# Work moved ahead of its phase: cross-attention's weights and first context, soft MoE's first norms, and the shared expert's turned rows

## The reference, cut to what matters

```python
x = x + tanh(g_xattn[0]) * ssm_attention(ctx, ctx, layernorm(x))          # phase 1
# phase 2 and 3: eight routed experts (top 2) and one shared expert
xn = layernorm(x)
moe = sum over e of ce[e] * (silu(xn @ gate[e]) * (xn @ up[e])) @ down[e]
shared = silu(xn @ s_gate_w + b) * (xn @ s_up_w + b) @ s_down_w + s_down_b
x = x + tanh(g_ffn[0]) * (moe + shared)
# phase 4: linear cross-attention, 16 heads
q, k, v = f(xn @ Wq.T), f(ctx @ Wk.T), ctx @ Wv.T                          # f(x) = x + 1 if x > 0 else exp(x)
x = x + tanh(g_xattn[1]) * ((q @ (k.T @ v)) / (q . sum(k)) * sigmoid(xn @ Wg.T + bg)) @ Wo.T
# phase 5: soft MoE, 16 experts of 128 slots
x_ln = layernorm(layernorm(x)) * gamma + beta      # the outer norm is the layer's own
logits = (l2norm(x_ln) * scale) @ l2norm(mu);  dispatch, combine = softmax over tokens-slots
x = x + tanh(g_ffn[1]) * combine @ (gelu(dispatch.T @ x_ln @ W1 + b1) @ W2 + b2)
```

## Time and profile before

| what | us |
|---|---|
| median of three runs | 1786.04 (1781.75 to 1788.67) |
| the profiled execution | 1787.78 |
| its span | 1786.1 |
| shared expert, from the first to the last of its own matmuls | 252 to 479 |
| routed experts, PE | 493 to 731.5 |
| cross-attention, PE | 743.6 to 1091.5 |
| soft MoE, PE | 1110.5 to the end |
| PE busy over the span | 1571.0 |

### The profile page before, as it was taken

How to read it: one execution, slowest core, us unless ns; L and a number is a source line. 1 busy time by engine, 2 the same in 40 slices (tenths; PEclk the granted TensorE clock), 3 DMA queues, 4 the chain that set the end, 5 groups by cost and what they waited for, 6 DMA issues and landing times. The chain is left out here.

```text
span 1786.1 us, 27541 instructions
## 1 busy us (share of the span) xinstructions
PE 1571.0 (88%) x9532; PEld 915.7 (51%) x9532; DVE 1094.1 (61%) x2223; ACT 752.3 (42%) x1386; POOL 513.2 (29%) x426
## 2 busy tenths in 40 slices
PE   4989948999799999579888874969999999999997
PEld 3878833444356666335444441445555555555554
DVE  7998845345622322368685855665766767675663
ACT  5442214343213322244343431555575656565462
POOL 0658814322324433333443322101202020101101
PEclk8999979999899999789999996989999999999999
DMA  9544544333575765641524125542341505142341
GB/s 206 141 120 150 157 151 150 115 128 128 182 187 124 183 178 136 225 152 60 159 85 146 55 88 211 210 94 54 77 89 42 129 8 121 28 101 53 66 88 44
DMA packets 274043, 215.19 MB, mean 120 GB/s; under 512 B 184514, under 2 KB 222914, under 8 KB 272274
## 3 DMA queue, kind: packets, MB, share of 16 engines
q1 hardware_dynamic: 233696, 153.58, 32.7%
q10 hardware_dynamic: 30978, 30.06, 5.6%
q0 software_dynamic: 9264, 30.15, 5.5%
HBM read 120.33 MB, written 49.63 MB: 95 GB/s over the span
## 5 line engine op out<-in xcount | busy, mean ns | idle before, releaser
L2031 POOL TENSOR_TENSOR s_h_lo<-s_h,s_h_hi 128x512 f16<-128x512 f32 x32 | 36.9, 1154 | 550.3 <-DVE s_h_hi L2242 550.3
L1218 DVE TENSOR_TENSOR e_h<-e_up,e_silu 128x352 f32<-128x352 f32 x39 | 20.5, 525 | 151.4 <-ACT e_silu L1177 151.4
L2260 PE MATMUL s_ring<-w_mu,s_xt_hi 128*128 128x512 f16 x256 | 98.4, 384 | 3.4 <-DVE s_xt_lo L2163 3.0
L2168 DVE TENSOR_REDUCE s_top<-s_lg 128x1 f32<-128x512 f32 x64 | 43.9, 686 | 89.1 <-ACT s_lg L2074 88.9
L2261 PE MATMUL s_ring<-w_mu,s_xt_hi 128*128 128x512 f16 x256 | 98.3, 384 | 0.0
L2262 PE MATMUL s_ring<-w_mu,s_xt_lo 128*128 128x512 f16 x256 | 98.0, 383 | 0.0
L2260 PE MATMUL s_acc<-w_w,s_g_hi 128*128 128x512 f16 x256 | 97.2, 380 | 0.1
L2262 PE MATMUL s_ring<-w_w,s_xt_lo 128*128 128x512 f16 x256 | 97.2, 380 | 0.0
L2260 PE MATMUL s_ring<-w_w,s_xt_hi 128*128 128x512 f16 x256 | 97.2, 380 | 0.0
L2261 PE MATMUL s_ring<-w_w,s_xt_hi 128*128 128x512 f16 x256 | 97.2, 380 | 0.0
L2261 PE MATMUL s_acc<-w_w,s_g_hi 128*128 128x512 f16 x256 | 97.1, 379 | 0.0
(11 more groups left out here) (378 smaller groups left out, 4809.7 us busy)
## 6 DMA issues: line engine op xcount, KB each, us to landing
expert_rows<-e_y SPq DMA_DIRECT2D x39, 256.0 KB, 2.0
a_part_in<-in_L_ffn_W ACTq DMA_DIRECT2D x32, 256.0 KB, 3.2
w_split<-a_part_q ACTq DMA_DIRECT2D x32, 256.0 KB, 2.5
w_w<-w_split SPq DMA_DIRECT2D x8, 1024.0 KB, 16.1
toep<-ssm_split ACTq DMA_DIRECT2D x14, 512.0 KB, 5.4
stage<-in_L_ffn_gate_w SPq DMA_DIRECT2D x8, 704.0 KB, 4.5
stage<-in_L_ffn_up_w SPq DMA_DIRECT2D x8, 704.0 KB, 5.2
c_rows<-in_ctx SPq DMA_DIRECT2D x8, 512.0 KB, 11.4
```

What stands on the lines that cost most here:

```text
L2031: nc.gpsimd.tensor_tensor(hp[1][:, n % 2, :], h32[:, :], hp[0][:, n % 2, :], ALU.subtract).then_inc(S["h_lo"], 1)
L2168: V.tensor_reduce(top[:, t, j:j + 1], lg[:, t, j * D:(j + 1) * D], AX.X, ALU.max).then_inc(S["top_done"], 1)
L2260: mm(out_, a[0], b_[0], start=first, stop=False)
```

## The change

Five things.

1. Shared expert: chunk 0 is as before. For chunks 1 to 3 PE no longer turns the rows and ACT and DVE no longer split turned blocks. The rows are normed, split untransposed into `xq` right behind the norm, and SP turns both halves with four DMA transposes (`xq_turned`) into `xt` once the last gate/up of the chunk before is done (`gu_done`). The store of `xq` comes behind them. PE waits for `xq_turned` ahead of gate/up, and for `bias_added` where it writes `tr`.
2. Experts: wk, wv, wq, wg, wo are loaded, split and stored as float16 pairs (`xw_split`) in 20 parts, one on every odd tile: ACT issues its load, copies and stores it, DVE subtracts. At tile 19 SP loads the first context into a tile that outlives the phases (`k.ahead.home`). `PERIOD` is 7.
3. Cross-attention: no WS. SP loads the five split weights, 1 MB each, the second context between the third and the fourth. The gathers are first on POOL. PE follows `begin`, all other engines `beside`, up to the first Q.
4. Chunk 3's Q/G stage takes in the two norms of soft MoE's batch 0 (N1a to N3b; SP loads its rows, gamma, beta and scale once the last context is turned).
5. Soft MoE starts with X; the loads of rows, gamma, beta, scale and the operations of N2f are gone.

```diff
+            def store_xn(c):
+                sp.wait_ge(xq_lo_done, (c + 1) * 4)
+                sp.dma_start(xn_d[:, c * 4:c * 4 + 4, :], xq.rearrange("p t q d -> p t (q d)")).then_inc(xn_stored, 16)
...
+                    sp.wait_ge(gu_done, (c + 1) * SK)
+                    for t in range(4):
+                        sp.wait_ge(xq_lo_done, (c + 1) * 4 + t + 1)
+                        sp.dma_start_transpose(xt[:, :, t * P:(t + 1) * P], xq[:, t, :, :].rearrange("p q d -> p (q d)")).then_inc(xq_turned, 16)
+                    store_xn(c + 1)
...
+            def split_rows(c, t):
+                if not t and c:
+                    act.wait_ge(xn_stored, c * 16)
+                    act.wait_ge(xq_turned, (c - 1) * 4 * 16)
+                act.wait_ge(normed, c * 4 + t + 1)
+                nc.scalar.activation(xq[:, t, 0, :], xn[:, t, :], ACT.Copy).then_inc(xq_hi_done, 1)
...
+                            if m == 0 and o == 0 and c and b == 0:
+                                pe.wait_ge(xq_turned, c * 4 * 16)
...
-        PEEL, FIRST, PERIOD = 9, 4, 8
+        PEEL, FIRST, PERIOD = 9, 4, 7
...
+                i = part_at(n)
+                if i is not None:
+                    v = i % PART_BUFS
+                    act.wait_ge(part_loaded[v], (i // PART_BUFS + 1) * 16)
+                    if i >= PART_BUFS:
+                        act.wait_ge(part_stored[v], i // PART_BUFS * 16)
+                    nc.scalar.activation(part_q[:, v, 0, :], part_in[:, v, :], ACT.Copy).then_inc(part_hi, 1)
+                    if i >= 1:
+                        store_part(i - 1)
+                    if i >= 1 and i + 1 < PARTS:
+                        load_part(i + 1)
...
+                if n == TILES // 2:
+                    sp.wait_ge(w.x1s_stored, NCH * 16)
+                    sp.dma_start(k.ahead.home[:, :, :], ctx.rearrange("(c k p) d -> p (c k) d", p=P, k=4)[:, 0:4, :]).then_inc(k.ahead.ctx_loaded, 16)
...
+        begin = ops(0, "TC", 4) + key(0) + key(1) + key(2) + key(3) + ops(0, "TX", 4)
+        beside = (ops(0, "TC", 4) + mixed(ops(0, "CB", 4), key(0) + key(1)) + ops(0, "NA", 1) + ops(0, "NB", 1)
+                  + ops(0, "TX", 4) + key(2) + key(3))
+        first_norm = [(0, op, 0) for op in ("N1a", "N1b", "N2a", "N2b", "N3a", "N3b")]
...
-            sp.dma_start(ctx_in[:, :, :], ctx_d[:, 0:4, :]).then_inc(ctx_loaded, 16)
             sp.dma_start(bg[:, :], bg_cols).then_inc(small_loaded, 16)
+            for n in range(5):
+                if n == 1:
+                    load_rows(0)
+                if n == 3:
+                    load_next(0)
+                sp.dma_start(halves[n].rearrange("p q k d -> p (q k d)"), xw_split[n]).then_inc(w_loaded[n], 16)
...
+                if c == NCH - 2:
+                    sp.wait_ge(c_turned, NCH * 4)
+                    sp.wait_ge(stored, c * 4 * 16)
+                    sp.dma_start(ah.x_ln, x3_d[:, 0:2, :]).then_inc(AS["x_loaded"], 16)
+                    for dst, src in ((ah.gam, gamma), (ah.bet, beta), (ah.scl, scale)):
+                        sp.dma_start(dst[:, :], src.partition_broadcast(P)).then_inc(AS["small"], 16)
...
-        F1a, F1b, F2a, F2b, F3a, F3b = normalised(1)
-        before = (F1a + F1b + F2a + one("N2f", 0) + ops("X", 0, 2, 1) + F3a + F3b + ops("L", 0, 4, 1) + ...
+        before = (ops("X", 0, 2, 1) + ops("L", 0, 4, 1) + ...
```

More of the change, by code:

```diff
@@ L753, in _ @@
                         split_piece(c, m)
[L754 to L757, removed]
+                        if c == 0:
+                            split_rows(0, m)
                     act.wait_ge(h_done, n + 1)
@@ L1233, in background @@
             def background(n):
+                i = part_at(n)
+                if i is not None:
+                    v = i % PART_BUFS
+                    dve.wait_ge(part_hi, i + 1)
+                    nc.vector.tensor_tensor(part_q[:, v, 1, :], part_in[:, v, :], part_q[:, v, 0, :], ALU.subtract).then_inc(part_lo, 1)
                 j = quarter_at(n, 5)
@@ L1303, in xattn_phase @@
         ln = LayerNorm(sb, sem, "x2")
-        wq, wg, wkv, wo = (tuple(sb(f"{n}_{q}", [P, KD, m], F16) for q in ("hi", "lo"))
-                           for n, m in (("wq", D), ("wg", D), ("wkv", 2 * D), ("wo", D)))
-        stage = sb("a_stage", [P, 2, 2, 2 * D])
+        halves = [sb(f"a_{n}", [P, 2, KD, D], F16) for n in ("wk", "wv", "wq", "wg", "wo")]
+        wk, wv, wq, wg, wo = ((h[:, 0], h[:, 1]) for h in halves)
         bg = sb("a_bg", [P, KD])
         mask = sb("a_mask", [P, 2 * P])
-        ctx_in, x2 = sb("a_ctx", [P, 4, D]), sb("a_x2", [P, X_BUFS, 4, D])
+        ah, AS = k.ahead, k.ahead.S
+        ctx_in, x2 = ah.home, sb("a_x2", [P, X_BUFS, 4, D])
         y_in = sb("a_y", [P, 4, 2, D])
+        waste = y_in[:, 0, 0, :].bitcast(F16).rearrange("p (t d) -> p t d", t=2)
         xn = sb("a_xn", [P, 4, D])
@@ L1348, in xattn_phase @@
         x1s_d, x3_d, ctx_d = (a.rearrange("(c k p) d -> p (c k) d", p=P, k=4) for a in (x1s, x3, ctx))
-        pieces = [(m, dst, b) for m, dst in ((wkv_t, wkv), (wq_t, wq), (wg_t, wg), (wo_t, wo)) for b in (0, 2)]
-        NP = len(pieces)
-        def staged(n):
-            cols = pieces[n][1][0].shape[2]
-            return stage[:, n % 2, :, 0:cols]
         def ops(c, op, count):
@@ L1380, in xattn_phase @@
         parts = iter(range(PARTS))
-        schedule = [o for at in schedule for o in ([at, (0, "P", next(parts))] if at[1] == "QF" or at[1] == "AT" and at[2] % 2 else [at])]
+        steady = [o for at in schedule for o in ([at, (0, "P", next(parts))] if at[1] == "QF" or at[1] == "AT" and at[2] % 2 else [at])]
         assert next(parts, None) is None
+        schedule = begin + steady
         w1_d = w1.rearrange("(j e) (p k) h -> j k p e h", j=NJ, k=KD)
@@ L1400, in xattn_phase, with run @@
                 home[at] = home[at[0], SECOND[at[1]], at[2]]
-        def run(step):
-            for at in schedule:
+        def run(step, first=beside):
+            for at in first + steady:
                 step(*at, home.get(at))
@@ L1523, in step @@
                     A(xt[0][:, :, n * P:(n + 1) * P], ring[:, bank, :].rearrange("p (k i) -> p k i", i=P), ACT.Copy).then_inc(x_hi, 1)
-                if op == "WS":
-                    act.wait_ge(w_loaded[n % 2], (n // 2 + 1) * 16)
-                    _, dst, b = pieces[n]
-                    A(dst[0][:, b:b + 2, :], staged(n), ACT.Copy).then_inc(w_hi, 1)
                 if op == "NA":
                     ln.root(nc, act, c)
+                if op == "N1a":
+                    ah.ln1.root(nc, act, 0)
+                if op == "N2a":
+                    ah.ln2.root(nc, act, 0)
+                if op == "N3a":
+                    act.wait_ge(combined, NCH * 4)
+                    for t in range(2):
+                        act.wait_ge(AS["xln_done"], t + 1)
+                        A(waste[:, t, :], ah.x_ln[:, t, :], ACT.Square, accum_out=ah.squares[:, t:t + 1]).then_inc(AS["squared"], 1)
+                    act.wait_ge(AS["squared"], 2)
+                    A(ah.l2[:, :], ah.squares[:, :], ACT.Sqrt).then_inc(AS["l2_done"], 1)
                 if op == "K":
@@ L1756, in step @@
                     last.then_inc(out_done, 1)
-            run(step)
+            run(step, begin)
 EXPERTS2, SLOTS2, HID2 = 16, 128, 128
@@ L1954, in _ @@
         def _(sp):
-            sp.dma_start(x_ln[:, :, :], x_d[:, 0:2, :]).then_inc(S["x_loaded"], 16)
-            for dst, src in ((gam, gamma), (bet, beta), (scl, scale)):
-                sp.dma_start(dst[:, :], src.partition_broadcast(P)).then_inc(S["small"], 16)
             def load_rows(b):
```

244 lines of the change are left out of this document (147 added, 97 removed).

## The result

The change takes the kernel from 1786.04 to 1769.08 us (medians; 1764.81 to 1771.85 over five runs). The ratio is 0.9903 with a 95% interval of 0.989 to 0.9916: faster by some 17 us, about half of the 32 us forecast, and 1 us above the range. The kernel before stands on record with five runs; their median and ends are the ones given above for three. It is also checked against the later profiles, because executions of this kernel differ more than its medians show.

The account below looks back on a forecast made before the run. PE, busy 88% of 1786.1 us, was taken as the bound, with holes at the seams between phases. Terms -7.1 + 1 - 16.8 + 3.5 - 12.2 = -31.6 gave 1754 from the median of 1786.04; range 1743 to 1768.

Parts of the forecast that it names:

- Shared expert (-7.1): Shared expert, chunks 1 to 3: dropping PE's transposes saves 2.35 us three times, 7.1 us; ends -7.1 and +1.
- Rival 1: Shared expert: DMA transposes land 0.7 to 3 us behind PE, three times; 1756 to 1763, say 1760; chance 0.12.
- Experts (+1): Experts: parts are covered, but period 7 makes ACT late for mu's quarters, 0.4 us twice; +1, ends 0 and +5.
- the bound of 2.3 for each wait: Experts, mu's third and fourth quarters: at the longest landing, 5.3 us, each wait costs 2.3 us.
- Rival 4: Experts: starved loads of parts hold ACT and the next tile's silu; slower than before, about 1838; chance 0.03.
- Cross-attention's start (-16.8): Cross-attention's start: K0 at 745, wv landing at 753, G0 ending at 786.5 instead of 803.25; bounds -20 and -11.
- Rival 2: Cross-attention's start: wv lands with the other queues' last byte, 754.4 or 756.5; total 1757; chance 0.13.
- Rival 5: Seams close only in part: mu's first MB waits at the new opening, K0 waits for wk to 750; 1764; chance 0.05.
- Norms (+3.5): Chunk 3's Q/G stage: the added norms delay the first attention step by 3.5 us; ends 0 and +7.
- Rival 3: Chunk 3's Q/G stage: six table switches cost more than 1.28 us each, adding 3 to 8 us; say 1762; chance 0.06.
- Soft MoE's start (-12.2): Soft MoE's start: mu's first MB is issued at once, first L at 1101 instead of 1113.15; bounds -9 and -13.4.
- the terms named for it: Whole kernel: unknowns reaching 10 us better: start -3, seam -1, norms -3.5, mu -1, and the runs' spread.

## Why the prediction was wrong in size

The forecast was 1754 with a range of 1743 to 1768, and the median is 1769.1: faster, as said, by half of what was said.

**Shared expert (-7.1): right.** Measured -6.8 in the first pair of traces. SP issues the four transposes at 314.26 (forecast 314.3), and gate/up starts at 322.86, where PE's transposes began before. Rival 1, late transposes, did not occur: PE has no wait on them at any of the three borders.

**Experts (+1): the mechanism was right, the landing was mis-sized.** The step was "with a landing of 3.4 us ... that is 0.4 us twice". The kernel before with a period of 7 measures exactly that, 0.36 twice. But the load was counted with the landings of a kernel without the parts. With them the piece takes 5.2 us, and the waits are 1.8 and 1.0 us, 2.3 and 0.8, and 5.8 and 2.0 in three profiles. Over seven profiles of kernels with period 7 and the changed shared expert, the stretch is 241.4 to 244.4 us, and once 250.2, where even the bound of 2.3 for each wait was too low. The term had no clock in it either: in three of the seven the first wait (2.27, 2.33 and 5.80 us) was followed by 4 to 8 us at a granted clock of about 0.6. Rival 4 had seen this direction and tied it to the wrong load: the parts' copies had cover enough, mu's quarters had not.

**Cross-attention's start (-16.8): the step that failed.** It reads "wv is the third MB of SP's queue; the third one before landed ... 12.8 us after the start ...: 753", that is 15.5 us behind an opening at 737.5. It came at 19.0 and 18.1. I counted what stood ahead of wv on its own queue and took the other queues for a small correction. The two runs that took bytes from other queues moved it to 16.7 and 15.2. Rival 2 had the working right: all bytes of the three queues, divided by the rate. At its lower rate it gave 756.5, which is 19.0 behind the opening; that this is the measured number to the tenth is luck, since the slices from 738 to 754 moved 378 to 412 GB/s and not 360, and those before 738 far less. The Trainium skill's rule that the DMA engines serve the queues in turn (DMA: Bandwidth & Descriptors, Queues, rings and completion order) agrees with these runs: bytes on other queues moved wv by 1 to 4 us. I held against it that no row showed two queues in this load, and gave it 0.13; but the earlier trace rows had all three at one total of 390 to 416 GB/s, which is itself the sign that they share. All behind wv followed, as the rival said, with Q0 at +45.4 against +41.6. Rival 5 did not occur: K0 stood at +8.2 against +7.5.

**Norms (+3.5): right in kind, 1.3 us short.** Measured +4.8. The walk had ACT's table loads and POOL's work. It missed that the squares wait for POOL in order (1.25 and 0.44 us) ahead of Q3's exponential. Rival 3, a hidden cost at each table switch, is not borne out: each load shows 1.28 us, and the three roots stand 1.29 to 1.42 us behind their load's start. With the drain that the Trainium skill puts on each switch (ScalarE: Activation LUTs, What ACT_TABLE_LOAD costs) the term would have been about 12 us; it was 4.8, and moving one of the three roots with its squares gave 3.5 back.

**Soft MoE's start (-12.2): right.** Measured -13.4. Of it 1.05 us comes back in the first L's: the slices of 4 us from the first L on (from 1088 and from 1113) have PEclk 0.50, 0.72, 1.00 in the change and 0.53, 1.00 before. PE stood 2.78 us ahead of them in place of 0.65, and the full clock comes a slice later.

**The sum.** The two large misses have one cause: a landing taken from a trace in which the queues were emptier than the change makes them. They add up to 6.8 of the 8.4 us between forecast and traces. The medians' gain is 6 us smaller again than the traces': the profiled execution of the change was 4.3 below its median, that of the kernel before 1.7 above. The waits on mu, different in each profile, are a part of that spread, as the 6.0 us between the two profiles of the change show stretch by stretch; the rest stays open. By the traces alone the result would be 1754 plus 8.4, 1762, which is inside the range; the range had put about 1 us on the spread between executions. Its lower end, 1743, is 11 below the forecast, where the terms named for it give 10.

## What to carry to other kernels

When a change adds transfers, don't take a landing from the old trace: add up the bytes of *all* queues issued before the last byte of the one awaited, and divide by the rate that the slices show. Here that is 6.0 MB at 378 to 412 GB/s from 734.71, and the 1.7 us that rival 2 allowed for the landing itself: 751.0 to 752.4, an estimate, against 753.2 measured. If a stretch starts by waiting for weights, put first whatever needs only the first of them (here 9.5 us, from the order of eight products and of DVE's work beside them). A period or look-ahead that is shortened in the same change as traffic is added must be checked against the longer landing, since either alone can look free.

## What the runs showed that I had not expected

- A PE wait of 2.27 us in the middle of a stretch at full clock was followed in one execution by a slice of 4 us at a granted clock of 0.57, and one of 2.33 us in another by 0.62. Waits of 1.81, 1.93, 2.03, 2.40 and 2.59 us at the same place in five other executions were not. So the length of the wait alone doesn't decide it.
- SP's issues of 1 MB loads themselves became long while those ahead were under way, 0.50 us and then 4.47 and 9.06 at the cross-attention's start, so the loads behind them can't be counted from the opening:

```profile
736.97 0.50 SPq L1485 DMA_DIRECT2D a_wv<-xattn_w_split  x1
...
738.86 4.47 SPq L1471 DMA_DIRECT2D a_x<-after_shared  x1
743.38 9.06 SPq L1485 DMA_DIRECT2D a_wg<-xattn_w_split  x1
```

- wk, the first of the five weights, landed after 4.9 to 7.7 us in nine profiles of kernels with the same issues ahead of it but for gathers or parts (7.7 and 5.3 in the two of the change itself). A single landing is not a constant to better than 2 us.
